# One perceiver layer on one Trainium2 core: the cross-attention loop in rounds of two steps, with the context loaded in 1 MB blocks

## What is computed

```python
q = (query @ Wq + bq).reshape(b, s, 16, 64)          # s = 128 rows, D = 512
k = (key @ Wk + bk).reshape(b, 2048, 16, 64)         # key = value = ctx, (4, 2048, 512)
v = (value @ Wv + bv).reshape(b, 2048, 16, 64)
logits = jnp.einsum('bshd,bShd->bhsS', q, k) / 8
weights = jax.nn.softmax(logits, axis=-1)
attn = jnp.einsum('bhsS,bShd->bshd', weights, v).reshape(b, s, 1024)
x1 = x + attn @ Wo + bo        # query is the layernorm of x; then self-attention, then the experts
```

## Time and profile before

| | us |
|---|---|
| median of 3 runs | 1391.34 (1388.34 to 1392.85) |
| the profiled execution, its own time | 1389.91 |
| its span, first to last instruction | 1388.1 |
| PE busy | 1342.5 (97%) |
| DVE, ACT, POOL busy | 882.4, 502.8, 179.1 |
| mean granted TensorE clock | 0.989 |

### The profile page before, as it was taken

One profiled execution on the slowest core, in us unless ns is written; L12 is line 12 of the kernel. 1 busy time (PEld: TensorE's weight loads), 2 busy tenths in 40 slices (PEclk: granted clock), 3 DMA queues, 4 the chain that ended last, 5 costly groups with the idle time before them and its releaser, 6 DMA issues.

```text
span 1388.1 us, 22386 instructions
## 1 busy us (share of the span) xinstructions
PE 1342.5 (97%) x9196; PEld 1095.4 (79%) x9196; DVE 882.4 (64%) x1280; ACT 502.8 (36%) x686; POOL 179.1 (13%) x140
## 2 busy tenths in 40 slices
PE   6999999999999999999999999999999987899999
PEld 5877888778878887887888777878887875688887
DVE  6426763695457448844763496457646457788779
ACT  4226541463135216521641264135313545312210
POOL 2211100140010004200100050011000500000030
PEclk9999999999999999999999999999999998799999
DMA  7401100240020004200100141010001321114300
GB/s 227 141 24 28 43 10 11 67 135 10 11 71 11 10 11 133 79 1 26 55 20 11 47 132 34 11 53 28 11 10 46 107 93 55 38 61 142 94 8 31
DMA packets 41107, 74.11 MB, mean 53 GB/s; under 512 B 6608, under 2 KB 10720, under 8 KB 39984
## 3 DMA queue, kind: packets, MB, share of 16 engines
q1 hardware_dynamic: 40096, 70.28, 16.4%
q0 software_dynamic: 912, 2.41, 0.6%
HBM read 69.53 MB, written 3.15 MB: 52 GB/s over the span
## 4 chain that ended last, share of the span: by engine, by line
PE 85%; DVE 9%; issue 2%; ACT 2%; DMA 1%; POOL 1%; SPq 0%; ACTq 0%; DVEq 0%
PE b_ps L1161 26%; PE b_ps L1183 21%; PE b_ps L474 9%; PE b_ps L1198 9%; PE b_ps L1233 7%; PE b_ps L500 3%; PE b_ps L397 3%; PE b_ps L1171 2%; PE b_ps L1259 2%; DVE b_mx L1474 1%; DVE b_prob L1492 1%; DVE b_sm L1501 1%; DVE b_ctxT L1390 1%; PE b_ps L1213 1%; DMA b_raw_v<-in_Wv 1%
## 5 line engine op out<-in xcount | busy, mean ns | idle before, releaser
L1183 PE MATMUL b_ps<-b_ctxT,wk 128*128 128x512 f32 x1536 | 385.8, 400 | 1.4 <-issue 1.4
L1161 PE MATMUL b_ps<-wv,b_ctxT 128*128 128x512 f32 x1536 | 361.2, 394 | 11.8 <-DVE b_ctxT L1390 11.7
L1161 PEld LDWEIGHTS b_ps<-wv,b_ctxT 128*128 128x128 f32 x1536 | 287.5, 189 | 75.8 <-issue 14.6
L1183 PEld LDWEIGHTS b_ps<-b_ctxT,wk 128*128 128x128 f32 x1536 | 280.9, 188 | 74.4 <-issue 12.0
L1361 ACT ACTIVATE b_kst<-b_ps,b_bkT 128x512 f32<-128x512 f32 x128 | 87.9, 687 | 452.0 <-PE b_ps L1183 451.0
L1408 DVE COPY b_V<-b_ps 128x512 f32<-128x512 f32 x128 | 88.3, 690 | 207.8 <-PE b_ps L1161 207.8
L1492 DVE TENSOR_TENSOR b_prob<-b_prob,b_ps 128x2048 f32<-128x2048 f32 x64 | 145.8, 2280 | 50.5 <-PE b_ps L1213 50.5
L1198 PE MATMUL b_ps<-b_q,b_kst 64*128 64x128 f32 x2048 | 148.7, 284 | 7.4 <-DVE b_mx L1474 7.4
L1198 PEld LDWEIGHTS b_ps<-b_q,b_kst 64*128 64x128 f32 x2048 | 124.5, 187 | 39.7 <-issue 36.0
L1371 ACT COPY b_prob<-b_ps 128x1024 f32<-128x1024 f32 x128 | 129.8, 1014 | 71.4 <-PE b_ps L1198 70.7
L1233 PE MATMUL b_ps<-b_prob,b_V 128*64 128x128 f32 x2048 | 138.6, 278 | 0.0
(11 more groups left out here) (206 smaller groups left out, 1203.1 us busy)
## 6 DMA issues: line engine op xcount, KB each, us to landing
stage<-in_ctx SPq DMA_DIRECT2D x64, 256.0 KB, 3.0
b_wo<-in_Wo SPq DMA_DIRECT2D x8, 1024.0 KB, 5.0
stage<-in_Wk SPq DMA_DIRECT2D x30, 256.0 KB, 2.7
stage<-in_Wv SPq DMA_DIRECT2D x28, 256.0 KB, 3.2
stage<-in_self_w SPq DMA_DIRECT2D x16, 256.0 KB, 2.8
t_raw<-in_q_proj SPq DMA_DIRECT2D x16, 256.0 KB, 4.5
t_raw<-in_k_proj SPq DMA_DIRECT2D x16, 256.0 KB, 3.2
t_raw<-in_v_proj SPq DMA_DIRECT2D x16, 256.0 KB, 3.5
```

The costliest lines, as they stand in the source:

```text
L1161: mm = nc.tensor.matmul(ps[:, G.bank[item]], ctxT[:, a, k, n * P:(n + 1) * P], wv[:, w, k], start=m == 0, stop=m == len(terms) - 1)
L1183: mm = nc.tensor.matmul(ps[:, G.bank["k", t]], wk[:, i % 2, w, k], ctxT[:, a, k, s * BANK:(s + 1) * BANK], start=m == 0, stop=m == len(ter ...
```

## The change

**Rounds.** The loop runs over rounds of two steps. PE does keys, keys, then scores, scores. In even rounds (the first two steps of a pair) it also turns and spreads the maxima of the pair before, and then weighs all four steps of the pair before that in one run. ACT and DVE loops are rewritten to match: both exponents of a pair are taken in the odd round, around the first key copy; DVE takes the last two maxima and both `below_max` in the even round, and `attention_out`, the first maximum and all sums in the odd one. Scores have four banks (2 to 5, two for each of two steps), keys, V and out products two (0 and 1).

**Values.** V is made 8 chunks at a time in two rounds (steps 4 and 6 of a half batch) instead of four at a time in four steps.

**Context.** The context comes in blocks of 512 rows, 1 MB, straight into the place of its `lo` half (`ctx_raw` lies over it), as soon as keys and values no longer need the block; `hi` is split from there and `lo` made in place. The four first chunks are loaded singly, in pieces of 512 bytes. Only Wk and Wv go through the ring. `CHUNK_STEPS` says when a chunk is split. Keys wait for `hi` first and for `lo` before their ninth matmul, and the order of the three passes is hi*hi, then the weights' lo, then the context's lo.

**Order of the rest.** The first out product of a batch moves from step 27 to step 31, the last round before a batch changes; those of the last batch and the pieces of the tail get other places: `sx` of the third batch and the first `pq` now follow in one round, and the softmax of the first self-attention rows, `sv1` and one `sp` stand ahead of the last out product.

```diff
+CHUNK_STEPS = (-3, -3, -3, -3, -2, -2, -1, -1, 0, 0, 0, 0, 1, 1, 1, 1)
...
-TAIL_STEPS = {114: "lr0", 116: "lr1 lr2", 122: "lr3 lr4 ln0", 123: "gate sx0 xl0", 124: "ln1", 125: "xl1 ln2 sx1",
...
+TAIL_STEPS = {114: "lr0 lr1", 116: "lr2 lr3 lr4 ln0", 121: "gate xl0 sx0", 122: "ln1 ln2", 123: "sx1 xl1", 126: "xl2",
+              127: "sx2 pq0 pq1", 129: "xf0 pk0 pk1 pk2 pk3", 130: "sv0 const pq2 pq3", 131: "sl00 sl01 sr00 sl02",
+              133: "sr01", 134: "sl03", 135: "sr02 sv1 sr03 sp00"}
...
-    LAG_WEIGH, RING = 8, 4
+
+    RING, SCORE_BANKS = 2, (2, 3, 4, 5)
...
-                self.products[half * h + 7 + n // SB].append(("v", h, n))
+                self.products[half * h + 4 + 2 * (n // 8)].append(("v", h, n))
...
-            groups = [(at + 27, 0, 4), (at + 42, 4, 8)]
+            groups = [(at + 31, 0, 4), (at + 42, 4, 8)]
             if b == NB - 1:
-                groups = [(at + 27, 0, 4), (at + 34, 4, 6), (at + 38, 6, 7), (at + 41, 7, 8)]
+                groups = [(at + 27, 0, 4), (at + 33, 4, 6), (at + 35, 6, 7), (at + 39, 7, 8)]
...
+        for b in range(1, NB + 1):
+            for n, t in enumerate(CHUNK_STEPS):
+                t += self.STEPS * b
+                (self.late[t // 2] if n < SB else self.splits[t]).append(("ctx", b, n))
...
-        loads = [(work[max(n - STAGE_SLOTS, 0)][0], 0, n, x) for n, x in enumerate(self.staged)]
+        loads = [(work[n - STAGE_SLOTS][0] + 2 if n >= STAGE_SLOTS else 0, 2, n, x) for n, x in enumerate(self.staged)]
         loads += [(SB * i - 3, 1, i, ("q", i)) for i in range(2, NB * NP)]
-        loads += [(half * k + (9 if k % 2 == 0 else 10), 2, k, ("wo", k)) for k in range(1, 2 * NB)]
-        self.loads = [x for *_, x in sorted(loads[NC:])]
+        loads += [(half * k + (11 if k % 2 == 0 else 12 if k == 2 * NB - 1 else 16), 3, k, ("wo", k)) for k in range(1, 2 * NB)]
+        loads += [(self.STEPS * b - SB + n // SB, 0, n, ("ctx", b, n)) for b in range(1, NB + 1) for n in range(0, NC, SB)]
...
-    LO_BY_DVE = [set(range(0, NC, 2))] * NB + [{0, 2, 4}]
+    LO_BY_DVE = [set(range(0, NC, 2))] + [{0, 2, 4, 6, 8, 9, 12, 13}] * (NB - 1) + [{0, 2, 4}]
...
+        ctx_at = nc.sbuf_base
         ctxT = sb("ctxT", [P, 2, C, S], F32R)
+        ctx_raw = at("ctx_raw", [P, C, S], ctx_at + 4 * C * S)
...
+            def load_chunk(b, n):
+                if b > 0:
+                    sp.wait_ge(k_psum, STEPS * b - SB + n // SB + 1)
+                    sp.wait_ge(v_psum, NC * (2 * b - 1) + n + SB)
+                if b == 0 and n < SB:
+                    src = ctx[0, 0].rearrange("p (c t) -> p c t", c=C)[:, :, n * P:(n + 1) * P]
+                    sp.dma_start(chunk_of(ctx_raw, n), src).then_inc(chunk_in[n], 16)
+                elif n % SB == 0:
+                    src = (ctx[b, n // SB] if b < NB else self_w[n // SB]).rearrange("p (c t) -> p c t", c=C)
+                    sp.dma_start(ctx_raw[:, :, n * P:n * P + BANK], src).then_inc(block_in[n // SB], 16)
...
-                    chunk_lo(pe, b, SB * s + SB - 1)
+                    pe.wait_ge(chi_done, NC * b + SB * s + SB)
                 if s == 0:
                     weight_lo(pe, ("wk", i))
-                terms = [(a, w, k) for a, w in ((0, 0), (1, 0), (0, 1)) for k in range(C)]
+                terms = [(a, w, k) for a, w in ((0, 0), (0, 1), (1, 0)) for k in range(C)]
                 for m, (a, w, k) in enumerate(terms):
+                    if (a, k) == (1, 0) and t % STEPS < SB:
+                        chunk_lo(pe, b, SB * s + SB - 1)
...
-                if t > 0:
-                    pe.wait_ge(s_out, t)
-                    pe.wait_ge(top_done, (SB - 1) * ((t - 1) // SB) + (t - 1) % SB)
+                if t < 2:
+                    pe.wait_ge(v_out, NC)
+                else:
+                    pe.wait_ge(s_out, t - 1)
+                    pe.wait_ge(top_done, (SB - 1) * ((t - 2) // SB) + (t - 2) % SB)
...
-            for t in range(LAST + 1):
-                w, i = t - G.LAG_WEIGH, (t - SB) // SB
-                if t < TOTAL:
-                    keys(t)
-                if t % SB == 1 and 0 <= i < NB * NP:
-                    turn_top(i)
-                if t % SB == 2 and 0 <= i < NB * NP:
-                    spread_top(i)
-                if 1 <= t <= TOTAL:
-                    scores(t - 1)
-                if w >= 2 and w % 2 == 0:
-                    weigh(w - 2)
-                    weigh(w - 1)
-                for item in G.products[t]:
+            for r in range(G.ROUNDS):
+                steps, weighed = (2 * r, 2 * r + 1), r // 2 - 2 if r % 2 == 0 else -1
+                complete = r // 2 - 1 if r % 2 == 0 else -1
+                if 2 * r < TOTAL:
+                    for t in steps:
+                        keys(t)
+                if 0 <= complete < NB * NP:
+                    turn_top(complete)
+                if 2 * r < TOTAL:
+                    for t in steps:
+                        scores(t)
+                if 2 * r < TOTAL and complete >= 0:
+                    spread_top(complete)
+                if weighed >= 0:
+                    for s in range(SB):
+                        weigh(SB * weighed + s)
+                if 2 * r >= TOTAL and 0 <= complete < NB * NP:
+                    spread_top(complete)
+                for item in G.items(r):
...
+            for r in range(G.ROUNDS):
+                exponents = r % 2 == 1 and 0 <= r - 3 < 2 * NB * NP
+                key_first = any(item[0] == "ctx" for item in G.splits[2 * r])
+                if exponents:
+                    exponent(r - 3)
+                if 2 * r < TOTAL:
+                    key_out(2 * r)
+                for item in G.splits[2 * r]:
                     split_hi(item)
-                for item in G.products[t]:
+                if exponents and not key_first:
+                    exponent(r - 2)
+                if 2 * r < TOTAL:
+                    key_out(2 * r + 1)
+                if exponents and key_first:
+                    exponent(r - 2)
+                for item in G.splits[2 * r + 1]:
+                    split_hi(item)
+                if 2 * r < TOTAL:
+                    scores_out(2 * r)
+                    scores_out(2 * r + 1)
+                for item in G.late[r]:
+                    split_hi(item)
+                for item in G.items(r):
...
+            for r in range(G.ROUNDS):
+                i = r // 2
+                if r % 2 == 0:
+                    if i - 1 in pairs:
+                        max_step(i - 1, 2)
+                        max_step(i - 1, 3)
+                        max_end(i - 1)
+                    chunks_rest(G.splits[2 * r])
+                    if i - 1 in pairs:
+                        max_rows(i - 1)
+                    chunks_rest(G.splits[2 * r + 1])
+                    if i - 1 in pairs:
+                        below_max(i - 1, 0)
+                        below_max(i - 1, 1)
+                else:
+                    if i - 2 in summed:
+                        attention_out(i - 2)
+                    if i in pairs:
+                        max_step(i, 1)
+                    chunks_rest(G.splits[2 * r])
+                    if i - 1 in summed:
+                        for s in range(1, SB):
+                            sum_step(i - 1, s)
+                        sum_end(i - 1)
+                    if i - 2 in pairs and i - 2 not in summed:
+                        attention_out(i - 2)
+                    chunks_rest(G.splits[2 * r + 1])
+                chunks_rest(G.late[r])
+                for item in G.items(r):
```

228 lines of the change are left out of this document (97 added, 131 removed).

## The result

Over four executions each, the changed kernel takes 1380.38 us (1379.57 to 1380.70), the kernel before 1390.0 us (1388.34 to 1392.85). The ratio is 0.9928, with a 95% interval of 0.9908 to 0.9947: 9.6 us or 0.7% faster. The forecast was 1373.8, in a range of 1360 to 1387: the sign was right, the gain a little over half of the one forecast.

What follows compares the result with a forecast made beforehand. PE was taken to bound the loop, chains through DVE the tail's first part. Terms of -15, -5.5, +1.5, +4.5 and -3 sum to -17.5 off the median of 1391.3, giving 1373.8 us, range 1360 to 1387.

Steps and rivals of the forecast that it cites:

- What bounds the kernel: Whole kernel: PE bounds the loop, chains through DVE the tail's first part; PE is busy 97% of the span.
- The joins: PE in the loop: joined keys save 0.38 and joined weighing 0.08 per pair, 15 us off, bounds 12 and 17.
- Rival B: PE in the loop: joined runs cost what single ones do, so 1389 us; chance 0.07.
- The chain under PE: Softmax chain in ordinary pairs: it ends 0.6 us before the turn needs it, so no wait and no term.
- Batch changes: Three batch changes in the loop: PE's waits fall from 7 to 1.5 us, 5.5 off, bounds 0 and 7.
- Third round: Third round, no weighing to cover pair 0's exponents: ACT about 2 us late, similar waits before, so 0.
- Start: First chunks loaded in 512-byte pieces: slower pieces, but no queue stalls on ring slots; 1.5 us more.
- The loop's end: Rounds 61 to 63: new waits of 1.4 on keys and 4.5 at the first pq, then slow clock; 4.5 us more.
- The tail: Tail's first part: DVE passes run earlier beside the last weighing; 3 us off, bounds -12 and +8.
- Rival A: Softmax chain in pairs without values: it becomes the bound, a wait in each pair, 1409 us; chance 0.07.
- C: Loop's end and tail: slow clock lasts longer and the tail's order misses DVE's pace, +10, 1384 us; chance 0.15.

Runs made afterwards that it cites:

- e4: Changed kernel with half of the weighing moved between the two key groups of every even round: 1375.53 us.
- e11: e10 with the turn of the maxima placed between the two steps' scores in even rounds: 1359.09 us.
- e1: Changed kernel with POOL's lo pass of the third value-weight part held until the pair's maxima are complete: 1375.32 us.
- e5: Changed kernel with all lo passes of context chunks of batches 1 to 3 on DVE, none on POOL: 1372.3 us.
- e2: Changed kernel; at batch changes POOL's chunk passes wait for the maxima and DVE takes max_rows ahead of its own chunk passes: 1380.61 us.
- e6: Changed kernel with pair 30's weighing ahead of the last turn and the first two pq behind it: 1378.59 us.
- e10: e9 plus three edits at the end: third norm later, reciprocal-root steps between value copies, work behind the third sx reordered: 1354.91 us.
- e7: Changed kernel with the first out product of batches 0 to 2 back at step 27: 1380.17 us.
- e8: Changed kernel with the edit of e1, e4's weighing only at batch changes, and DVE's first two new-batch chunk passes behind the first maximum: 1364.35 us.
- e9: e8 with all lo passes of context chunks on DVE as well: 1362.89 us.
- e3: Changed kernel with POOL's lo passes of Wk and Wv in the loop cut to a fraction of their columns: 1371.59 us.

## Why the prediction came out as it did

*What bounds the kernel.* Right: PE in the loop, and the joins came off its path.

*The joins, -15 (12 to 17).* Right in kind, too small: 0.88 a pair, 27 us. Keys (0.38) and weighing (0.15, at the upper bound rather than at 0.08) were priced; the joined scores, 4 * 1.09 against 2 * 1.98, or 0.4 a pair, were not, although has the 1.09. The change joins three kinds of runs and the sum counted two. The spread costs 0.09 more behind scores than behind keys. Rival B, and with it the reading of the Trainium skill (TensorE: Matmul & The Clock Gate, Back-to-back issue gap) on which it stood, is refuted twice: the same matmuls differ by 0.38 (e4) and 0.34 us a pair (e11) by their order alone.

*The chain under PE.* Of the 0.6 of slack 0.3 was there: in a quiet pair `max_end` is done at 180.2 and the turn starts at 180.49, 13.2 us into the pair. What failed is the sentence that passes on DVE follow each other at their mean durations, with POOL set aside as "beside". In seven pairs with a value weight POOL's pass lies on `max_end`: 5.7 us that the sum didn't have, shown by e1. The sign was in the trace of before, where it lay on sums that had time (timeline of all engines; L1505 takes 0.69 elsewhere):

```profile
286.20 1.56 POOL L1087 TENSOR_TENSOR b_ctxT<-stage,b_ctxT 128x512 fp32r<-128x512 f32 x1 [1.12 <-ACT b_ctxT L1299]
286.53 1.78 DVE L1505 TENSOR_TENSOR b_sm<-b_sm 128x512 f32<-128x512 f32 x1
```

*Batch changes, from 7 to 1.5.* The step that failed worst: 17 instead of 1.5. The forecast put `max_end` at T+17 and the turn at T+16.5 (T = 272.15). Measured are T+20.6 and, without the wait, T+18.1. PE itself is 1.6 late, by a wait of 0.67 at the scores and 0.76 inside the keys; the rest isn't traced. Of the 3.6 that `max_end` is late, 0.9 + 1.0 + 0.95 are the three passes stretched beside POOL, 0.6 is the residual of the out product, which the list left out though it had moved that product into the round. The wait of 1.26 at the spread is `max_rows` behind two stretched chunk passes, an order on DVE that the walk didn't follow past `max_end`. That POOL's passes are the cause of the stretching is shown by e1 and e5; that moving them alone doesn't help, by e2.

*Third round.* Waits of 0.73 and 0.24, against 0.63 and 1.31 before: 1.0 less, where 0 was forecast. *Start, +1.5.* It was -0.5; the 512-byte pieces cost nothing that shows: 48 values take 12.85 from their start at 11.93, before 13.51. That part wasn't tried by itself.

*The loop's end, +4.5.* Both new waits came, at their places, within 0.4 us. The slow clock behind the second came too: by e6 it cost 1.4 us, where 1.8 to 3 was put for it. Two waits of 0.67 (967.71) and 0.93 (1004.08) were missed: the steps of the reciprocal root ahead of the maxima on DVE. e10 took them away, and its 8.0 for a forecast of 7 says that such waits were on the path.

*The tail, -3 (-12 to +8).* The stretch behind the loop's end is 2.6 longer for a forecast of 3.9. It has the wait of 4.11, and PE is busy 1.4 longer with the same work at a clock of 0.93 instead of 0.95; so the new order of the tail brought about 3. Its size is read off as a remainder, not shown.

*The whole.* Errors of opposite sign: 12 us of gain in the joins and 3 in start and rest that weren't priced, against 23 us of waits in the loop (15.5 at the changes, 5.7 beside value weights, 1.6 at the reciprocal root), leave 8 of the 17 missing. That the number fell inside the range is partly luck, since the two largest terms were each off by more than 10. Of the parts of the change, only the joins (e4, e11) and the place of the out product (e7) were undone by themselves; what the order of the values and the loading in blocks bring isn't shown. Rival A had the right mechanism, the chain as the bound, but as something in every pair; it came in the pairs where POOL works. C, the likeliest rival, has nearly the right number (1384) and the wrong place: not the end and the tail, but the changes.

## What to carry over

When an order by rounds makes a chain thin, go through every link of it once more and ask what POOL does at that moment: in these traces a pass with both operands in SBUF takes 0.9 to 1.0 us longer beside one of POOL's. Work that is handed to POOL to relieve a busy DVE can cost more than it saves (0.9 for 0.69 here). Where a wait is fixed by another engine's chain, move work of the waiting engine ahead of it, even at the price of a join; and count every kind of run that a change joins. Don't take a wait's length for its whole price, either: behind some of them the clock falls, and whether that costs time depends on what waits next (e2, e6).

## What the runs showed of the hardware

**DVE and POOL shut each other out.** DVE's passes on SBUF alone take about 0.9 us longer beside a POOL pass of 1.27 (L1529 0.69 to 1.61, L1531 0.42 to 1.37, four chunk passes 2.49 to 6.08). It goes the other way too: POOL's pass at 281.54, which begins 0.2 behind the first of two sums, takes 2.18. Passes with an operand in PSUM keep their time: two `below_max` beside POOL's passes at 269.94 take 4.48, as elsewhere. A pass with one input (L1574, 0.29) took 1.19 beside one at 277.02. The Trainium skill (SBUF — State Buffer, SBUF: two separate sides) states it so: a GpSimd instruction and a VectorE one with two SBUF inputs, or in a two-port mode, share one pair of ports as an exclusive lock, for the whole instruction. The trace agrees: L1529 at 263.17 begins 0.22 behind a POOL pass of 1.29 (262.95), which then has 1.07 left, and takes 0.92 longer. Of handing work from DVE to GpSimd the Trainium skill (Perfetto Trace Analysis, Optimizing Scalar/DVE Operations) says that it might not help; e5 has the number for it, 8.1 us the other way.

**A run of scores has an end of 0.1 us,** like that of keys: 1.09 for one step's, 1.98 for two.

**Behind a wait the granted clock falls at some places and not at others.** In the changed kernel the turn waits 2.59, 2.61 and 2.60 at the three changes, each time after keys that had kept PE busy. Behind the first wait the granted clock is 1.00 and 32 entries of scores take 1.98 us; behind the second it is 0.51 and they take 3.24, behind the third they take 3.50. In e2 the same happens behind two of three waits of 1.70. In e4, e5, e8, e9 and e10, whose turns wait at most 1.21 in the loop, no joined scores take over 2.2. What decides between the places isn't shown.

**The mean granted clock isn't the same in each execution.** e6 took 1374.42 at 0.990 and 1381.24 at 0.983, with four others between; e3 1368.21 at 0.990 and 1376.46 at 0.979; the changed kernel shows 0.982 to 0.985, the joined weighing undone (e4) 0.986 to 0.988. Where in the span the others differ isn't recorded. In the profiled executions of the changed kernel and of e10 the loop has 1.00 as a whole and the rest 0.93 and 0.95. So differences of 2 us between kernels whose tails wait aren't told apart here by four to six executions.
